# The decoder layer's fourth expert pair: its product of gate and up moved from VectorE to GpSimd, with new places for all stages

## The reference

```
x  = layernorm(x + mamba(x))          # 256 inner channels, 16 states, 4 taps
x  = layernorm(x + retention(x, ctx)) # q, k, v, xpos rotation, decay mask
x  = layernorm(x + moe(x))            # 16 experts of width 64, top 2, and a shared one

def mamba(x):
    x_b, z  = split(x @ W_in)
    xc      = silu(conv(x_b))                       # 4 taps along the sequence
    dt, B, C = split(xc @ W_xproj)
    delta   = softplus(dt @ W_dt + b_dt)
    h_t     = exp(delta * A) * h_(t-1) + delta * B * xc   # a scan along each sequence, for 16 states
    y       = sum over states(h_t * C) + D * xc
    return (y * silu(z)) @ W_out

def moe(x):
    scores, chosen = top_k(x @ router_w.T + router_bias, 2)
    combine = softmax(scores) at the chosen experts, 0 elsewhere
    hidden  = silu(x @ gate_e) * (x @ up_e)         # for each expert e
    return sum over e(combine_e * hidden_e @ down_e) + shared expert
```

## Time and profile before

| | |
|---|---|
| median of 3 runs | 1137.81 us (1137.12 to 1139.98) |
| the profiled execution | 1136.04 us |
| its span | 1134.1 us |
| PE busy | 1030.5 us, 91% of the span |
| DVE busy | 1048.2 us, 92% |
| ACT busy | 991.2 us, 87% |
| POOL busy | 989.4 us, 87% |
| granted TensorE clock | 0.975 of full speed over the span |

### The profile page before, as it was taken

One profiled execution on the slowest core, in us unless ns is written; L12 is line 12 of the kernel. 1 busy time (PEld: TensorE's weight loads), 2 busy tenths in 40 slices (PEclk: granted clock), 3 DMA queues, 4 the chain that ended last, 5 costly groups with the idle time before them and its releaser, 6 DMA issues. The chain is left out here.

```text
span 1134.1 us, 18240 instructions
## 1 busy us (share of the span) xinstructions
PE 1030.5 (91%) x5831; PEld 732.6 (65%) x5831; DVE 1048.2 (92%) x1458; ACT 991.2 (87%) x2159; POOL 989.4 (87%) x608
## 2 busy tenths in 40 slices
PE   4786888999999999999999999999999999989897
PEld 2464656676766767676676767666676767666665
DVE  2999999999999999999999999999999999999521
ACT  6779798999999999999999999999999999898442
POOL 0577798999989898998989899898989999898854
PEclk9678899999999999999999999999999999999999
DMA  6544454555546465555646465554645555552221
GB/s 161 210 155 160 166 171 176 181 186 177 193 169 197 160 191 184 187 179 178 207 152 203 164 197 187 177 191 168 213 171 191 191 179 186 178 186 106 84 94 52
DMA packets 84111, 194.49 MB, mean 171 GB/s; under 512 B 17288, under 2 KB 47936, under 8 KB 67632
## 3 DMA queue, kind: packets, MB, share of 16 engines
q1 hardware_dynamic: 84016, 193.33, 50.7%
HBM read 179.14 MB, written 5.77 MB: 163 GB/s over the span
## 5 line engine op out<-in xcount | busy, mean ns | idle before, releaser
L937 POOL TENSOR_TENSOR read<-state,bc_all 128x1024 f32<-128x1024 f32 x256 | 605.2, 2366 | 92.4 <-DVE state L811 85.5
L811 DVE TENSOR_TENSOR_SCAN state<-decay,drive_bank 128x512 f32<-128x512 f32 (+1 forms) x464 | 594.2, 1315 | 1.9 <-issue 0.2
L761 ACT ACTIVATE decay<-delta,a_neg 128x252 f32<-128x252 f32 x1024 | 422.5, 494 | 0.9
L803 DVE TENSOR_TENSOR drive_bank<-dx_bank,bc_all 128x512 f32<-128x512 f32 (+1 forms) x496 | 329.9, 702 | 2.6 <-DMA bc_all<-bc_dram 2.5
L373 PEld LDWEIGHTS y_bank<-ident,read 128*128 128x128 f32 x2048 | 239.8, 145 | 88.2 <-POOL read L937 47.4
L373 PE MATMUL y_bank<-ident,read 128*128 128x128 f32 x2048 | 275.8, 279 | 22.1 <-POOL read L937 21.9
L982 POOL TENSOR_TENSOR hid<-gu,comb_all 128x512 f32<-128x512 f32 (+1 forms) x136 | 165.0, 1214 | 17.7 <-DVE gu L897 12.4
L364 PEld LDWEIGHTS down_bank<-down_w,hid 128*128 128x128 f32 x1024 | 127.0, 192 | 30.4 <-issue 27.5
L731 ACT ACTIVATE silu<-bank 128x512 f32<-128x512 f32 (+1 forms) x153 | 87.8, 576 | 57.8 <-PE bank L364 55.1
L364 PE MATMUL down_bank<-down_w,hid 128*128 128x128 f32 x1024 | 135.8, 277 | 1.5 <-POOL hid L982 1.5
L364 PE MATMUL bank<-x2T,up_w 128*128 128x512 f32 (+1 forms) x272 | 132.1, 570 | 0.5 <-ACT silu L731 0.5
(11 more groups left out here) (127 smaller groups left out, 1356.0 us busy)
## 6 DMA issues: line engine op xcount, KB each, us to landing
bc_all<-bc_dram SPq DMA_DIRECT2D x128, 1024.0 KB, 4.9
comb_all<-comb_dram SPq DMA_DIRECT2D x240, 128.0 KB, 4.1
x_in<-in_x_dram SPq DMA_DIRECT2D x15, 256.0 KB, 5.4
ctx_in<-in_ctx_dram SPq DMA_DIRECT2D x15, 256.0 KB, 5.5
k_pair<-k_pair SPq DMA_DIRECT2D x30, 128.0 KB, 2.5
q_pair<-q_pair SPq DMA_DIRECT2D x30, 128.0 KB, 2.1
out_dram<-y_out SPq DMA_DIRECT2D x15, 256.0 KB, 6.0
comb_all<-comb_dram SPq DMA_DIRECT2D x32, 64.0 KB, 2.6
```

The lines of the kernel that those rows point to most:

```text
L761: done = e.activation(seqs(decay_t[j % DECAYS][:, i, h, :])[:, :, 1:T], seqs(delta[c % 2][:, h, sub * SUB:(sub + 1) * SUB])[:, :, 1:T], AC ...
L803: e.tensor_tensor(drive_bank[:, a:b, :, :], dx_bank[:, :, :].unsqueeze(1).to_broadcast(shape), bc_all[group % BC_BUFS][:, 0, PAIR * i + a: ...
L811: e.tensor_tensor_scan(states(state_t[j % STATE_BUFS], a, b), states(decay_t[j % DECAYS], a, b), states(drive_bank, a, b), 0.0, ALU.mult, ...
L937: e.tensor_tensor(read_t[j % READS][:, :, :, :], state_t[j % STATE_BUFS][:, :, :, :], bc_all[group % BC_BUFS][:, 1, PAIR * i:PAIR * (i + 1 ...
```

## The change

`POOLED = 3` names the fourth pair. Its `gu` is no longer made by DVE. A new ACT stage `pooled_copy` copies the pair's up product from its bank to the pair's `gu` buffer, and POOL multiplies silu into this buffer in place (line 1001 of the changed kernel, at the tick of the pair's `gu`). `hid` of the pair waits for that, DVE's count of `gu` is seven to a chunk, and the bank comes free with the copy. Beside that, nearly every place in `AT`, `EXP_AT` and `LAST_EXP_AT` is another one.

```
+POOLED = 3
+BY_DVE = PAIRS - 1
...
-    "router_mm": [(128, 102)],
+    "router_mm": [(130, 101)],
...
+    "pooled_copy": [(161, 176)],
...
+        def gu_done(c, pair):
+            return at(c, pair - (pair > POOLED), BY_DVE)
...
-                    bank.free = (S["up_copy"], at(c)) if index == 0 else (S["gu"], at(c, index - 1, PAIRS))
+                    if index == 0:
+                        bank.free = (S["up_copy"], at(c))
+                    elif index - 1 == POOLED:
+                        bank.free = (S["pooled_copy"], at(c))
+                    else:
+                        bank.free = (S["gu"], gu_done(c, index - 1))
...
+                for c in due(tick, "pooled_copy"):
+                    w.wait_ge(S["up_mm"], at(c, POOLED + 1, TILES))
+                    w.wait_ge(S["hid"], at(c, POOLED - 2, PAIRS))
+                    copy(gu[(POOLED + 1) % 2][:, 0:width(c)], bank_of["up", c, POOLED + 1][:, 0:width(c)]).then_inc(S["pooled_copy"], 1)
...
                 for c, pair in due(tick, "gu"):
...
+                    if pair != POOLED:
...
+                for c, pair in due(tick, "gu"):
+                    if pair == POOLED:
+                        total = TILES * c + POOLED + 1
+                        made = gu[(POOLED + 1) % 2][:, 0:width(c)]
+                        w.wait_ge(S["silu"], total + 1)
+                        w.wait_ge(S["pooled_copy"], at(c))
+                        e.tensor_tensor(made, silu[total % 2][:, 0:width(c)], made, ALU.mult).then_inc(S["pooled"], 1)
```

More of the change, by code:

```diff
@@ L64 @@
[L64 to L68, removed]
-    "q_copy": [(79, 71)],
[L70 to L82, removed]
@@ L101 @@
[L101 to L105, removed]
+    "xT_mm": [(-49, -47)],
+    "tap_mm": [(-39, -42)],
+    "xb_mm": [(-41, -44)],
+    "proj_mm": [(-34, -31)],
+    "dt_mm": [(-19, -21)],
+    "ctxT_mm": [(53, 25)],
+    "k_mm": [(65, 67)],
+    "v_mm": [(60, 68)],
+    "out_mm": [(69, 67)],
+    "q_mm": [(79, 68)],
+    "r1_var_mm": [(83, 71)],
+    "score_mm": [(94, 88)],
@@ new lines @@
+    "normed3": [(206, 308)],
+    "xc0": [(-39, -41)],
+    "xc1": [(-34, -32)],
+    "delta": [(-19, -18)],
+    "top_tanh": [(131, 106)],
+    "tap1": [(-39, -42)],
+    "tap2": [(-37, -40)],
+    "tap3": [(-36, -38)],
+    "rstd2": [(108, 97)],
+    "rstd3": [(197, 302)],
+    "k_rot": [(70, 67)],
+    "k": [(81, 79)],
+    "q_rot": [(85, 81)],
+    "q": [(91, 81)],
+    "ret": [(102, 82)],
+    "bc_store": [(-30, -41)],
+    "k_swap": [(65, 37)],
+    "q_swap": [(77, 67)],
+    "comb_store": [(132, 114)],
@@ L106 @@
+    "x_load": [(-97, -54)],
+    "ctx_load": [(-37, -50)],
+    "store": [(230, 288)],
+    "z_mm": [(10, 27), (37, -8)],
+    "gate_z": [(10, 27), (41, 25)],
+    "y_gated": [(39, 65), (69, -14)],
+    "yT_mm": [(57, 55), (69, 12)],
+    "yT": [(58, 55), (66, -49)],
+    "dx": [(-17, -17), (24, -14)],
+    "dx_bank": [(-6, -7), (30, -76)],
     "gate_mm": [
-        (135, 134), (141, 137), (142, 157), (151, 161), (157, 189), (163, 203), (176, 226), (178, 243), (179, 286)],
+        (138, 139), (141, 141), (142, 162), (149, 164), (157, 203), (163, 208), (176, 220), (177, 223), (178, 248)],
@@ L114 @@
+    "gu": [(143, 144), (148, 157), (156, 163), (161, 189), (172, 237), (181, 248), (186, 252), (186, 286)],
+    "hid": [(145, 150), (151, 156), (157, 159), (167, 189), (177, 207), (181, 233), (185, 280), (190, 294)],
     "down_mm": [
[L115 to L118, removed]
@@ L888, in _ @@
                 for c, pair in due(tick, "gu"):
[L889 to L896, removed]
-                    e.tensor_tensor(gu[index % 2][:, 0:width(c)], silu[total % 2][:, 0:width(c)],
-                                    bank_of["up", c, index][:, 0:width(c)], ALU.mult).then_inc(S["gu"], 1)
+                    if pair != POOLED:
+                        index = pair + 1
+                        total = TILES * c + index
+                        w.wait_ge(S["silu"], total + 1)
+                        w.wait_ge(S["up_mm"], total + 1)
+                        if index == 2:
+                            w.wait_ge(S["shared"], at(c))
+                        else:
+                            w.wait_ge(S["hid"], at(c, index - 3, PAIRS))
+                        e.tensor_tensor(gu[index % 2][:, 0:width(c)], silu[total % 2][:, 0:width(c)],
+                                        bank_of["up", c, index][:, 0:width(c)], ALU.mult).then_inc(S["gu"], 1)
         @block.gpsimd
```

79 lines of the change are left out of this document (35 added, 44 removed).

## The result

The changed kernel takes 1158.95 us, the median of 4 runs (1156.51 to 1163.79), beside 1138.18 for the kernel before: a ratio of 1.0186, with a 95% interval from 1.0148 to 1.0224. It is slower by 21 us where 3 us of gain were forecast, and outside the range.

The account below looks back on a forecast made before the run. DVE, 99.4% busy, was taken to bound the kernel; after the change a 64.80 us loop would. Terms of -4.3 (chunks), -0.6 (early chunks), +1.8 (start) and 0 (end) made -3.1: 1134.7 us by the median, range 1130.0 to 1142.0.

Parts of the forecast that it names:

- DVE's 0.60 us: DVE loses one gu product a chunk, 0.60 us, so DVE alone would need 64.53 instead of 65.13.
- the third rival: SP issues bc_all's load for steps 6 and 7 late, behind comb_all; landing at 8.5 gives 1141.2 us; chance 0.10.
- The swap of k: Transfer ahead of POOL's rotation of k: lands some 2.5 us after its issue, 0.9 in time.
- the fourth rival: POOL becomes the bound because the rotation of k does not fit its gap: +9 to +16, about 1147 us; chance 0.12.
- The rotation moves into the gap.: The 2.30 us rotation of k goes into POOL's 2.67 us idle time ahead of step 9's read.
- another one of the same engine: GPSIMD engine-selection rule: elementwise products belong on VectorE, GpSimd being about half as fast; rows gave 1.23 against 0.60.
- The loop of 64.80.: Loop through DVE's scan, POOL's run, PE's products, gate_z and next scans: sets a chunk's pace, 0.33 us gained.
- The router's term: router_mm on PE, now ahead of step 7's transposes, adds 0.81 us to the loop.
- The start.: a_exp between the first chunk's two silus, with two table loads, delays the start by 1.8 us (bounds 0.5 and 2.8).
- The end.: Last stretch, PE's with the same products: 0 us change taken (bounds -1.3 and +2.5).
- the figure by the drain: By the skill page's 1380 ns drain at each switch, two table loads cost 2.8 us more, giving 1137.6.
- the first rival: The loop does not bind and DVE's 64.53 us sets the pace: 1131.2 us; chance 0.17.

Follow-up runs that it names:

- e1: Changed kernel with the last pair's load of comb_all behind the load of bc_all for steps 6 and 7, as before the change: 1143.37 us.
- e3: Changed kernel with e1's alteration and the swap of k issued ahead of the load of bc_all: 1181.39 us.
- e12: Changed kernel with the swap of k ahead of the load of bc_all and the rotation waiting for the pick, comb_all's load left as changed: 1153.52 us.
- e6: e3 with one wait added, the rotation of k on POOL waiting for DVE's pick of the chunk before: 1141.24 us.
- e7: e3 with the rotation of k behind the read of step 9 on POOL, as before the change: 1153.13 us.
- e2: Changed kernel with only the swap of k ahead of the load of bc_all: 1188.89 us; rule cited: two-SBUF-input VectorE and SBUF-reading GpSimd instructions lock shared ports.
- e9: e6 with a_exp ahead of both silus at the start and the last chunk's load of x further ahead on SP: 1137.24 us.
- e10: e6 with router_mm's old place, ahead of step 6's transposes, in all chunks but the last: 1144.35 us.
- e13: e9 with the fourth pair's product on DVE again and no copy of up on ACT: 1139.76 us.
- e11: e10 with a_exp ahead of both silus at the start: 1141.93 us.

## Why the prediction was wrong

The step that failed is the rotation of k in POOL's gap, and with it the load for steps 6 and 7: two transfers that were taken to land in time did not, and the gap was not free. The parts one by one:

**DVE's 0.60 us.** Right: seven products on DVE, 64.36 us busy in 67.2.

**What SP issues ahead of the load for steps 6 and 7** (the third rival). Right in its mechanism, and its time of issue nearly so: 35.5 us after the end of step 10's scan were reckoned, 36.2 are in the trace (599.65 to 635.87). The step that failed is the landing, and with it the chance of 0.10: I judged this load by the median of its line, 4.9 us. By the DMA views of single issues it landed in 9.2 us in the changed kernel, and in 8.4 already in the kernel before, where it was issued early enough; in e1 it landed in 7.8 (in this order):

```profile
bc_all<-bc_dram SPq DMA_DIRECT2D x1, 1024.0 KB, 9.2
bc_all<-bc_dram SPq DMA_DIRECT2D x1, 1024.0 KB, 8.4
bc_all<-bc_dram SPq DMA_DIRECT2D x1, 1024.0 KB, 7.8
```

Over the 15 full chunks the load for steps 6 and 7 has medians of 8.7, 6.5 and 7.8. In e1 it has the same half MB of `ctx` and `x` directly ahead, but not the two stores directly behind, that of `bc_dram` and that of the output; in the kernel before it has the stores behind and a quarter of a MB ahead. So both neighbourhoods go with a landing above 4.9, and what each of them costs is not told apart.

**The swap of k** (the fourth rival). "The swap of k lands some 2.5 us after its issue" was the failing term: it lands in 4.8, since the copy that I moved forward in the sum brings the swap to just behind a load of 1 MB, which goes out when the read of step 7 ends. I reckoned when the swap would be issued, and not what stands ahead of it then. e3 confirms it: ahead of the load it lands in 2.0. In the prediction's own terms the rotation had to start by 581.71. In the changed kernel it starts at 595.67, which is 582.27 in those times (step 9's scan ends 13.40 later): 0.56 late, and of the size of the 0.45 a chunk that e12 gets back.

**Rivals priced one by one.** At the third I let DVE give 0.27 us, at the fourth I had a margin of 0.9. Both lie in one loop: rotation, POOL's run, the fourth pair's `hid`, SP, the load, the drive of step 6, the next pick. What one used up the other had no more.

**"The rotation moves into the gap."** This is the deeper fault, and it would have stood with the swap in time. I took POOL's 2.67 us of idle time as free. It is the time in which DVE's pick must not meet the rotation; with the rotation in it a chunk takes 68.2 (e3), somewhat under 1 us of it with the clock, and the late swap of the changed kernel even kept the rotation clear of the pick by half a us in most chunks (595.67 against 594.88 + 0.23). e6 and e7 settle this. The prediction did not weigh the rule that is named at e2; it weighed another one of the same engine.

**The loop of 64.80.** With the two transfers and the pick out of the way (e6, e9) the pace is 65.24 to 65.26, as before, not 64.80. In e6 the rotation after the pick and the read of step 9 are done at 589.4, some 0.2 after the scan of step 10 lets the next read start (586.85 + 2.32 + 0.08 = 589.25): a piece that the sum lacked. The router's term was wrong (e10). The rest, some 0.3 us, stays open: PE is busy 63.48 us of a chunk of e6, 1.3 more than before for the same products, by the windows. It is 63.31 in e13 too, so that this goes with the new places and not with the moved product.

```profile
582.20:647.50 65.30, 63.48 (x362) 44.10 (x360) 64.28 (x90) 62.33 (x135) 62.82 (x38) 1.00 0.54 183
```

**The start.** +1.8 was forecast, +3.3 is there at the first pick. The two loads and `a_exp` come in as reckoned, and then ACT waits for PE:

```profile
13.74 1.28 ACT L649 ACT_TABLE_LOAD   x1
15.04 0.23 ACT L649 ACTIVATE a_exp<-a_log 128x32 f32<-128x32 f32 x1
15.28 1.28 ACT L730 ACT_TABLE_LOAD   x1
16.58 0.42 ACT L730 ACTIVATE xc<-conv 128x256 f32<-128x256 f32 x1
19.01 0.38 ACT L609 ACTIVATE proj<-bank 40x256 f32<-40x256 f32 x1 [2.02 <-PE bank L371]
...
31.92 0.59 ACT L609 ACTIVATE dx_bank<-dx 128x512 f32<-128x512 f32 x1
```

What the sum left out is PE's clock. PE stood idle for 3.84 us until the second silu was done, and then took 1.93 us for products that took 1.06 before (PE's timelines after and before, then the window after):

```profile
17.05 1.93 PE L371 MATMUL bank<-xc,w_xproj 128*40 128x256 f32 x4 [3.84 <-ACT xc L730]
14.00 1.06 PE L364 MATMUL bank<-xc,w_xproj 128*40 128x256 f32 x4 [0.87 <-ACT xc L718]
15.70:29.40 13.70, 11.20 (x20) 5.06 (x21) 2.60 (x5) 10.67 (x20) 1.26 (x1) 0.50 0.84 224
```

In that window the granted clock is 0.50, the lower level of 1.2 GHz; from 14 to 26 us the kernel before had 1.00. From the second silu to the first decays ACT's chain takes 7.9 us (16.58 to 24.50) instead of 5.9 (13.54 to 19.42). The place of `a_exp` alone does not settle the clock: with it ahead of both silus the same products take 1.06 us in e9 and 1.93 in e11. So `dx_bank` is copied at 31.92 instead of 29.7, and the row sums of `w_qkv` start at 38.42 instead of 36.2, by DVE's timeline:

```profile
38.42 0.29 DVE L856 TENSOR_REDUCE row_sum<-w_qkv 128x1 f32<-128x128 f32 x1 [1.16 <-ACT shared_w L609]
```

After each of the two loads the next activation stands 0.02 us behind (13.74 + 1.28 and 15.04; 15.28 + 1.28 and 16.58). The drain that the Trainium skill, "ScalarE: Activation LUTs", section "What ACT_TABLE_LOAD costs", adds to a switch is not seen in these rows.

**The end.** 0 was taken; +6.3 - 1.8 = +4.5 is measured in the profiled execution. It is no price of the end's places alone: the late transfers play into these two chunks, and so does the clock. The chunk ahead of the last pick but two, by the windows, in the changed kernel and in e6, with nearly the same places at the end (the kernel before takes 64.89 at a clock of 1.00):

```profile
993.57:1064.67 71.10, 64.33 (x360) 47.12 (x358) 64.10 (x90) 60.90 (x135) 62.73 (x38) 0.93 0.49 164
973.75:1040.23 66.48, 60.21 (x360) 44.08 (x358) 64.01 (x90) 60.95 (x135) 62.75 (x38) 1.00 0.53 176
```

The profiled execution of e9, whose transfers are mended, has 70.65 at 0.95 there, and is 5 us above e9's median. So some 4 us of this chunk go with a fall of the clock, or with what went ahead of the fall; no run separates these, and by the medians not every execution seems to have them. The changed kernel's profile, too, is 5 us above its median.

Two of the prediction's sums are off by a tenth or a half: the figure by the drain is 1137.5 and not 1137.6, and the first rival with half of the lower bound at the end is 1130.5 and not 1130.0. Nothing hangs on either.

## What to carry to other kernels

Ask of an idle gap what it keeps apart before putting work into it: an engine that shows no wait can be held inside its own instructions, and only their durations tell (a 128x4 difference of 2.31 us). A transfer's landing is read from that transfer's own issue and from what stands beside it in the queue at its new time, not from the median of its line. And delays that lie in one loop are summed along the loop, not priced as rivals.

## What the runs showed of the hardware

DVE instructions with two SBUF operands (`above`, `lead`, `rank`) that came just behind the start of POOL's 2.35 us rotation stood until its end, at 2.3 to 2.4 us instead of 0.16 to 0.23. `above` kept its 0.22 beside POOL's `rstd` of 1.01 us, and scans and drives, which read one operand from PSUM, keep their 1.21 and 1.27 us beside POOL's reads. A swap of 128 KB lands in 2.0 us ahead of a load of 1 MB, and in 4.8 when issued 0.7 us behind it. The Trainium skill, "DMA: Bandwidth & Descriptors", section "Two DMAs through the same engine are not ordered", has it that descriptors within one queue of one DMA engine start in order but are pipelined; the two landings fit this. At a granted clock of 0.50 a matrix product with `w_xproj` took 0.63 us, where it took 0.38 at 1.00.
